# Experts ranked by token count on chip, their matrices fetched in rank order, and the extra items moved to places nine to eleven

## The chip, the core and the metric

The kernel runs on one NeuronCore of a Trainium2 chip. Its engines are TensorE (PE, with its weight loads PEld), VectorE (DVE), ScalarE (ACT), GpSimd (POOL) and SyncE (SP); each takes its own instructions strictly in the order of the program and waits at semaphores. The metric is the device time of one execution in microseconds.

## What is computed

2048 rows of 512 numbers are normalised and go through one of four experts each; the expert follows from the row's token id. All three matrices of an expert are the same 512 x 512 context matrix. Behind that stands a second normalisation and a block with low-rank routed adapters, which the change leaves alone.

```python
def _L0_xattn_ref(hidden_states, token_ids, Wg, Wu, Wd):
    ...
    expert_ids = jnp.minimum(tid // tokens_per_expert, E - 1)
    out = jnp.zeros_like(hidden_states)
    for e in range(E):
        g = jax.nn.silu(jnp.einsum('bsd,fd->bsf', hidden_states, Wg[e]))
        u = jnp.einsum('bsd,fd->bsf', hidden_states, Wu[e])
        y = jnp.einsum('bsf,df->bsd', g * u, Wd[e])
        out = jnp.where((expert_ids == e)[..., None], y, out)
    return out
...
x = x + jnp.tanh(g_xattn[0]) * _L0_xattn_ref(_layernorm(x, axis=-1), itok_BxS_13_99985, ctx_2048, ctx_2048, ctx_2048)
x = x + jnp.tanh(g_ffn[0]) * _L0_ffn_ref(_layernorm(x, axis=-1), ...)
```

## The kernel before, in words

**Items.** The kernel sorts the rows by expert on chip (a counting sort on VectorE, with matrix products on TensorE for the sums over partitions and for the permutation) and gathers them as 16 tiles of 128 rows. A tile in which another expert begins needs a second pass with that expert's matrix; there are three such extra passes, so 19 items in all. The extra items stand at places 1 to 3 (`EXTRA_AT = 1`), so that items 0 to 3 have the fixed keys 0 to 3, one expert each.

**An item's path.** GpSimd gathers its rows (`gather`); VectorE takes their statistics (`first_rows`, later `item_stats` and `item_aggregate`); GpSimd makes root and centre of them (`item_root`); ScalarE normalises (`norm`). The row block h is split into a high and a low half of 16 bits and transposed: for items 0 to 4 by TensorE (`transpose_h` there, then `hT_hi` on ScalarE and `hT_lo` on VectorE), from item 5 on by a DMA of SyncE's queue (`h_hi`, `h_lo`, then `transpose_h` of SyncE). TensorE computes z = h * ct in twelve matmuls (hi by hi, lo by hi, hi by lo). ScalarE makes `silu_of` z, VectorE multiplies (`activate`), both split the result (`act_hi`, `act_lo`), SyncE's queue transposes it (`transpose_act`), and TensorE computes y = act * ct in twelve matmuls (`product_y`). VectorE adds y to the rows (`add_product`). Here z0 is the z product of item 0, y0 its y product. From item 6 on a loop runs z of item q and y of item q-2 in turn, and each engine does its part of the items around q in one round.

**The matrices.** Each of the four matrices (1 MB in f32) comes through `ct_stage` and is split in two halves of rows into 16-bit high and low parts (`ct_hi` on ScalarE, `ct_lo` on VectorE), after a scale that follows from the sum of its squares (`ct_scales` on VectorE). For the first matrix ScalarE squares and sums; for the others TensorE multiplies the matrix by itself (`gram`) and VectorE takes the trace (`trace`). A product with ones (`total`) sums over partitions.

**The order at the start.** SyncE loads ids, gates and three matrices at once, the fourth after the first four gathers were issued. VectorE makes the row index (`row_index`) and two short tables and then goes into a handwritten order of calls, from `ct_scales` of the first matrix to the loop; the gate mask (`gates_of_rows`) stands in the middle of it. GpSimd issues four gathers and then alternates roots and gathers; `scale_tables`, which makes the scales of all items from the four matrices' scales, stands once, behind root 6. The weights W of the second block are loaded in the ramp, squared in rounds 8 and 9, scaled (`w_exponent`, `w_scales`) in rounds 10 and 11 and split from round 12 on. An extra item's product is stored over its gathered rows and added to its tile in rounds 11 to 13 (`add_extra`), where VectorE reads the tile's number from a table into a register (`target_of`, a `value_load`).

TensorE's own order at the start, several calls to a line, where the prediction walks along:

```python
transpose_h(0); keep_warm(WARM_BETWEEN); z_hi_by_hi(0, 0); z_lo_by_hi(0, 0); z_hi_by_lo(0, 0)
transpose_h(1); gram(3); z_hi_by_hi(1, 1); z_lo_by_hi(1, 1); transpose_h(2); z_hi_by_lo(1, 1)
...
z_hi_by_hi(2, 2); transpose_h(3); z_lo_by_hi(2, 2); z_hi_by_lo(2, 2); product_y(0, 0); transpose_h(4); z_hi_by_hi(3, 3)
...
product_y(1, 1); product_z(5, keys[5]); product_y(2, 2); product_y(3, 3)
```

## Time and profile before

| what | value |
|---|---|
| median of 3 runs | 199.44 us (199.04 to 199.58) |
| the profiled execution, its own time | 198.81 us |
| its span, first to last instruction | 197.1 us |
| mean granted TensorE clock | 0.971 of full speed |
| TensorE busy | 185.5 us (94%) |
| VectorE busy | 142.5 us (72%) |
| ScalarE busy | 111.9 us (57%) |
| GpSimd busy | 116.2 us (59%) |
| chain that ended last | TensorE 81%, GpSimd 7%, VectorE 5%, issue 3% |

The chain of waits follows the work that ended last back to the start; "issue" is time in which an engine waited for nothing that the profile shows. Times of rows are from the span's start. The 1.7 us between the execution's time and its span lie around the instructions. An engine's idle time outside the chain costs nothing by itself, but sets when others can start.

### The profile page before, as it was taken

The numbers are of one execution on the slowest core, as the hardware profiler recorded it, in microseconds if no ns is written. First come the engines' busy times: TensorE is split into PE (matmuls) and PEld (weight loads), VectorE is DVE, ScalarE is ACT, GpSimd is POOL, SyncE is SP. The second block draws the span as 40 slices with busy tenths as digits, with TensorE's granted clock in tenths as the row PEclk, the third lists the DMA queues.
The fourth block names the chain that finished last, engine by engine and source line by source line (L and its number), as shares of the span: only waits on it lengthen the run. The fifth ranks groups of instructions, "written<-read, shape, count | busy, mean of one in ns | idle before, by whom it ended". The sixth has DMA issues, their size and how long they took to land.

```text
span 197.1 us, 3762 instructions
## 1 busy us (share of the span) xinstructions
PE 185.5 (94%) x1085; PEld 107.6 (55%) x1085; DVE 142.5 (72%) x409; ACT 111.9 (57%) x208; POOL 116.2 (59%) x190
## 2 busy tenths in 40 slices
PE   6699899899999999999999999999999999999970
PEld 2374435344444454444444446667778777787750
DVE  5959889968866666998888664676767777676370
ACT  4563769465357765267665456354756777567310
POOL 5578856882566662233377654376776767765441
PEclk9966999999999999999999999999999999999995
DMA  2988426889799998456569997565989989889951
GB/s 86 365 297 276 148 74 168 219 167 185 145 212 214 180 222 188 92 105 117 106 137 216 205 239 200 85 175 151 114 131 131 139 125 124 135 124 131 127 91 72
DMA packets 59827, 31.63 MB, mean 161 GB/s; under 512 B 53105, under 2 KB 53105, under 8 KB 59810
## 3 DMA queue, kind: packets, MB, share of 16 engines
q1 hardware_dynamic: 54994, 18.58, 46.5%
q0 software_dynamic: 4816, 12.85, 30.5%
q8 instruction: 8, 0.13, 0.3%
q14 instruction: 9, 0.07, 0.1%
HBM read 10.71 MB, written 7.86 MB: 94 GB/s over the span
## 4 chain that ended last, share of the span: by engine, by line
PE 81%; POOL 7%; DVE 5%; issue 3%; ACT 1%; POOLq 1%
PE actT_ps L783 8%; PE y_ps L783 8%; PE ffn_b L783 6%; PE z_ps L783 6%; PE ffn_b L765 6%; PE ffn_a L765 6%; POOL xg L431 4%; PE actT_ps L788 4%; PE y_ps L788 4%; PE z_ps L788 3%; PE ffn_b L788 3%; PE ffn_b L769 3%; PE z_ps L765 3%; PE ffn_a L769 3%; PE y_ps L765 3%
## 5 line engine op out<-in xcount | busy, mean ns | idle before, releaser
L502 POOL DMA_INDIRECT out<-scaled,row_index x14 | 22.4, 1603 | 10.5 <-ACT scaled L611 4.9
L431 POOL DMA_INDIRECT xg<-x_rows,row_index x19 | 21.8, 1149 | 5.5 <-issue 4.2
L394 POOL TENSOR_SCALAR var_eps<-item_stats_t 128x1 f32<-128x1 f32 x19 | 6.9, 366 | 30.3 <-DVE item_stats_t L1116 30.0
L566 ACT ACTIVATE act_split<-act 128x512 f16<-128x512 f32 x19 | 11.9, 628 | 15.8 <-DVE act L1141 15.7
L765 PE MATMUL ffn_a<-w_split,hT 128*128 128x316 f16 x88 | 18.8, 298 | 0.0
L765 PE MATMUL ffn_b<-w_split,hT 128*128 128x314 f16 x88 | 18.4, 296 | 0.0
L444 POOL DMA_INDIRECT out<-xg,row_index x14 | 14.7, 1053 | 5.3 <-issue 3.0
L574 ACT ACTIVATE h<-xg,item_centre,item_rstd 128x512 f32<-128x512 f32 x18 | 14.5, 803 | 5.2 <-POOL item_centre L404 5.1
L783 PE MATMUL actT_ps<-ct_split,actT 128*128 (+1 forms) x72 | 17.0, 379 | 0.0
L783 PE MATMUL y_ps<-ct_split,actT 128*128 (+1 forms) x72 | 17.0, 379 | 0.0
L596 ACT ACTIVATE expd<-logits,neg_max 128x6 f32<-128x6 f32 x16 | 4.8, 300 | 19.8 <-DVE neg_max L1287 19.8
L587 ACT ACTIVATE h<-xg,centre,rstd 128x512 f32<-128x512 f32 x16 | 12.8, 802 | 3.5 <-POOL centre L491 3.5
L1146 DVE TENSOR_TENSOR act_split<-act,act_split 128x512 f16<-128x512 f32 x19 | 13.0, 683 | 1.3 <-ACT act_split L566 1.3
L1112 DVE BATCH_NORM_STATS2 bn<-xg 128x6 f32<-128x512 f32 x19 | 13.0, 687 | 1.0 <-DMA xg<-x_rows,row_index 1.0
L484 POOL TENSOR_SCALAR var_eps<-stats 128x1 f32<-128x1 f32 x16 | 6.8, 423 | 11.7 <-DVE stats L1119 11.6
L783 PE MATMUL ffn_b<-ct_split,hT 128*128 x56 | 13.2, 379 | 0.0
L783 PE MATMUL z_ps<-ct_split,hT 128*128 x56 | 13.2, 379 | 0.0
L397 POOL TENSOR_TENSOR item_rstd<-var_eps,minus_half 128x1 f32<-128x1 f32 x19 | 11.5, 603 | 1.6
L769 PE MATMUL ffn_b<-w_split,hT 128*128 128x314 f16 x44 | 11.8, 296 | 0.0
L769 PE MATMUL ffn_a<-w_split,hT 128*128 128x316 f16 x44 | 11.7, 296 | 0.0
L559 ACT ACTIVATE silu<-ffn_b,z_scale 128x512 f32<-128x512 f32 x9 | 6.1, 682 | 9.8 <-PE ffn_b L788 6.6
L783 PEld LDWEIGHTS y_ps<-ct_split,actT 128*128 128x128 f16 x72 | 7.0, 98 | 8.5
(227 smaller groups left out, 474.2 us busy)
## 6 DMA issues: line engine op xcount, KB each, us to landing
ct_stage<-ct SPq DMA_DIRECT2D x4, 1024.0 KB, 7.7
w_stage<-w_ffn SPq DMA_DIRECT2D x4, 315.0 KB, 3.7
hT<-h_split SPq DMA_TRANSPOSE x30, 3.7
xg<-x_rows,row_index POOLq DMA_INDIRECT x19, 3.9
actT<-act_split SPq DMA_TRANSPOSE x19, 3.8
out<-xg,row_index POOLq DMA_INDIRECT x16, 2.7
up_stage<-w_up SPq DMA_DIRECT2D x1, 224.0 KB
out<-scaled,row_index POOLq DMA_INDIRECT x14
```

The source lines that it names most:

```text
L431: nc.gpsimd.indirect_dma_start(cols(xg, q), None, x, bass.IndirectOffsetOnAxis(row_index[:, q:q + 1], 0)).then_inc(x_landed[q], 16)
L444: nc.gpsimd.indirect_dma_start(out, bass.IndirectOffsetOnAxis(row_index[:, q:q + 1], 0), cols(xg, q), None).then_inc(x2_stored, 16)
L502: nc.gpsimd.indirect_dma_start(out, bass.IndirectOffsetOnAxis(row_index[:, q:q + 1], 0), scaled[t % 3][:], None, compute_op=ALU.add).then_ ...
L566: nc.scalar.activation(act_split[q % 2][:, 0:D], act[:], ACT.Copy).then_inc(act_hi_ready, 1)
L574: nc.scalar.activation(h[:], cols(xg, q), ACT.Identity, bias=column(item_centre, q), scale=column(item_rstd, q)).then_inc(h_ready, 1)
L587: nc.scalar.activation(h2[:], cols(xg, tile_position(l)), ACT.Identity, bias=centre[:], scale=rstd[:]).then_inc(h2_ready, 1)
L765: nc.tensor.matmul(ps, h2T[turn][:, k], rhs(part), start=(k == 0 and part == 0), stop=False)
L769: return nc.tensor.matmul(ps, h2T[turn][:, KC + k], rhs(0), start=False, stop=(k == KC - 1))
L783: nc.tensor.matmul(ps[:], lhs[:, k], expert_weights(key, k, part), start=(k == 0 and part == 0), stop=False)
L788: last = nc.tensor.matmul(ps[:], lhs[:, KC + k], expert_weights(key, k, 0), start=False, stop=(k == KC - 1))
L1112: nc.vector.bn_stats(bn[:], cols(xg, q)).then_inc(bn_ready, 1)
L1146: tt(act_split[q % 2][:, D:], act[:], act_split[q % 2][:, 0:D], ALU.subtract).then_inc(act_lo_ready, 1)
```

## The change

The kernel ranks the four experts by their number of rows and sorts the rows in that order, so that items 0 to 3 all belong to the largest expert and items 4 to 7 to the two largest (`ITEM_GROUPS`). Only the first matrix is needed before item 4, the second before item 8, the third and the fourth from items 9 and 10 on. SyncE loads W first, waits for the order, reads the experts' numbers into registers and loads the matrices in rank order, in halves and spread over the ramp. All squares are ScalarE's; `gram` and `trace` are gone. The extra items stand at places 8 to 10, and their products are added straight onto their tiles, whose numbers VectorE loads into three registers ahead of its first row. W's squares, exponent and scales move to the start, the gate mask too. `scale_tables` runs three times, once for each group of items, each time as soon as its matrices have scales. GpSimd's order of gathers and roots changes. Stores of finished tiles begin some rounds earlier. `ct_total(s)` waits for both squares of matrix s and sums them on TensorE.

The core of the diff:

```diff
-WARM_UP = (2, 1, 2, 5)
-WARM_BETWEEN = 3
-EXTRA_AT = 1
-EXTRA_ADD_AT = 11
+WARM_UP = (8, 8)
+WARM_BETWEEN = 1
+EXTRA_AT = 8
...
+        ITEM_GROUPS = ((0, 4, (0,)), (4, EXTRA_AT, (0, 1)), (EXTRA_AT, ITEMS, (0, 1, 2, 3)))
...
+        def ranks_split_by(q):
+            if q < 4:
+                return 1
+            return min(S, max(2, q - EXTRA_AT + 2))
...
@@ SyncE @@
+            for k in range(KC):
+                load_w(k)
+            sp.wait_ge(order_ready, 1)
+            expert_of_rank = [order_of(0)]
+            load_ct(0, 0)
+            load_ct(0, 1)
+            expert_of_rank += [order_of(s) for s in range(1, S)]
...
+            sp.wait_ge(first_gathered, 1)
+            load_ct(1, 0)
+            load_ct(1, 1)
...
             transpose_act(0)
-            load_w(0)
-            load_w(1)
+            load_ct(2, 0)
             transpose_act(1)
-            load_w(2)
+            load_ct(2, 1)
             transpose_h(5)
             transpose_act(2)
             transpose_act(3)
...
@@ GpSimd, in scale_tables(group), and its main order @@
+                pool.wait_ge(z_scale_ready, len(ranks))
                 pool.wait_ge(tables_ready, 1)
...
             gather(0)
             gather(1)
-            gather(2)
-            gather(3)
             nc.gpsimd.memset(gathered_mark[:], 0.0).then_inc(first_gathered, 1)
             item_root(0)
+            gather(2)
+            item_root(1)
+            gather(3)
+            scale_tables(0)
+            item_root(2)
             gather(4)
-            item_root(1)
+            item_root(3)
             gather(5)
+            scale_tables(1)
+            item_root(4)
             gather(6)
...
@@ ScalarE @@
+            w_square(0)
+            w_square(1)
+            ct_square(0, 0)
+            ct_square(0, 1)
             ct_hi(0, 0)
             ct_hi(0, 1)
             hT_hi(0)
...
+            act_hi(1)
             hT_hi(3)
+            ct_square(1, 1)
             norm(4)
             silu_of(2)
+            act_hi(2)
             hT_hi(4)
+            ct_hi(1, 0)
             norm(5)
             h_hi(5)
+            ct_hi(1, 1)
             silu_of(3)
...
+                if q == 6:
+                    ct_hi(2, 0)
+                    ct_square(3, 1)
...
@@ TensorE @@
+            z_hi_by_hi(2, 0)
             transpose_h(3)
+            z_lo_by_hi(2, 0)
+            z_hi_by_lo(2, 0)
+            ct_total(1)
             product_y(0, 0)
+            z_hi_by_hi(3, 0)
             transpose_h(4)
+            z_lo_by_hi(3, 0)
+            z_hi_by_lo(3, 0)
+            product_y(1, 0)
             pe.wait_ge(tables_ready, 1)
             keys = {q: key_of(q) for q in (4, 5)}
...
                 product_z(q, key)
+                if q == 7:
+                    ct_total(3)
...
@@ VectorE @@
+            dve.wait_ge(tables_ready, 1)
+            targets = [dve.value_load(target_table[0:1, bass.ds(q, 1)], min_val=0, max_val=ITEMS - 1)
+                       for q in range(EXTRA_AT, EXTRA_AT + EXTRAS)]
...
+            w_exponent()
+            w_scales()
+            first_rows(0)
+            ct_scales(0)
+            first_rows(1)
+            first_norm()
             ct_lo(0, 0)
+            hT_lo(0)
             ct_lo(0, 1)
...
+                if q == 9:
+                    ct_lo(3, 0)
+                    ct_lo(3, 1)
```

## Rows read from the trace of the kernel before

**Rows 1.** Windows: start and end, length, busy time by engine, PEclk, DMA share, GB/s.

```profile
19.67:40.98 21.31, 19.34 (x106) 9.44 (x106) 19.16 (x41) 14.57 (x21) 15.58 (x25) 1.00 0.56 154
40.98:190.00 149.02, 148.89 (x881) 88.76 (x880) 107.99 (x302) 87.35 (x176) 84.89 (x131) 1.00 0.83 152
11.90:18.60 6.70, 6.49 (x31) 3.93 (x31) 5.24 (x13) 3.32 (x4) 5.61 (x7) 0.50 0.78 234
```

**Rows 2.** The chain of waits in order of time: start, length, what.

```profile
35.89 0.98 issue
...
51.72 1.73 PE z_ps L783 x8
...
72.78 1.75 PE z_ps L783 x8
```

**Rows 3.** Timeline: the Gram product between the first z products, on TensorE.

```profile
23.18 1.08 PE L735 MATMUL ffn_b<-ct_stage 128*128 128x128 bf16 x16
```

**Rows 4.** Timeline: from the counting matmuls to the first z product.

```profile
4.39 0.21 DVE L1066 TENSOR_TENSOR begun<-ffn_a,tile_starts 128x45 f32<-128x45 f32 x1 [0.41 <-PE ffn_a L706]
...
7.00 2.13 DVE L1086 TENSOR_SCALAR lo_onehot<-iota_row,slot_lo 128x128 f16<-128x128 f16 x12
...
9.52 0.18 DVE L1089 CAST row_index<-ffn_a 128x19 int32<-128x19 f32 x1 [0.38 <-PE ffn_a L715]
...
10.01 0.18 DVE L1096 CAST key_table<-item_key 128x19 int32<-128x19 f32 x1
...
14.54 0.69 DVE L1112 BATCH_NORM_STATS2 bn<-xg 128x6 f32<-128x512 f32 x1 [0.97 <-DMA xg<-x_rows,row_index]
...
19.67 2.76 PE L794 MATMUL z_ps<-ct_split,hT 128*128 128x512 f16 x12
```

**Rows 5.** Timeline of VectorE: the gate mask, first and last; the weight steps likewise.

```profile
38.68 0.21 DVE L1042 SCALAR_TENSOR_TENSOR reached<-ffn_a,row_slot 128x57 f32<-128x57 f32 x1
...
39.58 0.23 DVE L1104 TENSOR_SCALAR gate_mask<-gate_mask,gates_t 128x19 f32<-128x19 f32 x1
...
75.03 0.13 DVE L1177 COPY w_total<-ffn_a 128x1 f32<-128x1 f32 x1
...
82.31 0.15 DVE L1193 COPY hw<-w_scale 128x1 f32<-128x1 f32 x1
```

**Rows 6.** By line: register loads, VectorE's and TensorE's queue; ns min/median/max.

```profile
L1161 DVEq TENSOR_LOAD <-target_table x3: 450/741/778, 77.0 to 86.5; - x3
L1161 DVEq FUSED_REGOPS  x3: 190/190/216, 77.8 to 87.3; - x3
...
L799 PEldq TENSOR_LOAD <-key_table x30: 296/310/1046, 34.7 to 118.4; - x30
```

**Rows 7.** GpSimd: gathers by line and landing; centres (timeline); scale table (groups).

```profile
L431 POOL DMA_INDIRECT xg<-x_rows,row_index x13: 942/1159/1872, 10.0 to 57.5; - x13
...
DMA to landing us min/median/max: 3.4/4.4/5.9
...
20.66 1.11 POOL L404 TENSOR_SCALAR item_centre<-item_stats_t,item_rstd 128x1 f32<-128x1 f32 x1
...
25.50 0.26 POOL L404 TENSOR_SCALAR item_centre<-item_stats_t,item_rstd 128x1 f32<-128x1 f32 x1
...
L412 POOL TENSOR_SCALAR z_scale_of<-item_key,z_scale 128x15 f32<-128x15 f32 x4 | 1.4, 362 | 0.0
```

**Rows 8.** Groups, 19 to 52 us: count, busy us, mean ns, idle before.

```profile
L1008 DVE SCALAR_TENSOR_TENSOR ct_split<-ct_stage,ct_scale,ct_split 128x1024 f16<-128x1024 f32 x6 | 7.6, 1267 | 0.0
L574 ACT ACTIVATE h<-xg,item_centre,item_rstd 128x512 f32<-128x512 f32 x7 | 5.6, 806 | 2.3 <-POOL item_centre L404 2.2
L540 ACT ACTIVATE ct_split<-ct_stage,ct_scale 128x1024 f16<-128x1024 f32 x4 | 4.6, 1139 | 0.3 <-DVE ct_scale L1023 0.3
L566 ACT ACTIVATE act_split<-act 128x512 f16<-128x512 f32 x6 | 3.7, 625 | 3.1 <-DVE act L1141 3.0
L548 ACT ACTIVATE hT<-hT_ps 128x512 f16<-128x512 f32 x5 | 3.0, 590 | 4.0 <-PE hT_ps L774 4.0
L1141 DVE SCALAR_TENSOR_TENSOR act<-ffn_b,act_scale,silu 128x512 f32<-128x512 f32 x3 | 2.2, 750 | 1.4 <-ACT silu L559 1.4
```

**Rows 9.** By line: SyncE's transposes of act, ns of issue; landing in us.

```profile
L310 SPq DMA_TRANSPOSE actT<-act_split x19: 1231/1233/2109, 27.9 to 121.0; - x19
...
DMA to landing us min/median/max: 3.2/3.8/5.3
```

More of the change, by code:

```diff
@@ L266, in build_block, with group_of, fixed_key @@
         Z_TOP = 18
-        W_SPLIT_AT = W_SCALE_AT + 2
+        W_SPLIT_AT = 10
         W_TOP = 14
+        ITEM_GROUPS = ((0, 4, (0,)), (4, EXTRA_AT, (0, 1)), (EXTRA_AT, ITEMS, (0, 1, 2, 3)))
+        def group_of(q):
+            return len([first for first, last, ranks in ITEM_GROUPS if first <= q]) - 1
+        def fixed_key(q):
+            if q < 4:
+                return 0
+            return q - EXTRA_AT + 1 if EXTRA_AT <= q < EXTRA_AT + EXTRAS else None
+        def ranks_split_by(q):
+            if q < 4:
+                return 1
+            return min(S, max(2, q - EXTRA_AT + 2))
         S_TOTAL, S_INVERSE, S_W = 0, 1, 2
@@ L554, in silu_of @@
                     act_e.wait_ge(act_ready, q)
-                if q < S:
-                    act_e.wait_ge(z_scale_ready, q + 1)
-                elif q == S:
-                    act_e.wait_ge(z_table_ready, 1)
-                nc.scalar.activation(silu[:], z_banks[q % 2][:], ACT.Silu, scale=column(z_scale, q)
-                                     ).then_inc(silu_ready, 1)
+                key = fixed_key(q)
+                if key is None:
+                    act_e.wait_ge(z_table_ready, group_of(q) + 1)
+                    scale = column(z_scale, q)
+                else:
+                    act_e.wait_ge(z_scale_ready, key + 1)
+                    scale = column(rank_z_scale, key)
+                nc.scalar.activation(silu[:], z_banks[q % 2][:], ACT.Silu, scale=scale).then_inc(silu_ready, 1)
             def act_hi(q):
@@ L743, in total, with ct_total @@
                 last.then_inc(ct_totalled, 1)
-            def total_of(first, count):
-                return squares_ps[:, TOTALS_AT + first:TOTALS_AT + first + count]
-            pe.wait_ge(ct_squared, 2)
-            total(first_total_ps[:, 0:1], ct_squares[:, 0:1], ct_squares[:, S:S + 1])
-            gram(1)
+            def ct_total(s):
+                pe.wait_ge(ct_squared, 2 * s + 2)
+                total(squares_ps[:, TOTALS_AT + s:TOTALS_AT + s + 1], ct_squares[:, 2 * s:2 * s + 1],
+                      ct_squares[:, 2 * s + 1:2 * s + 2])
+            pe.wait_ge(rows_ready, 1)
+            pe.wait_ge(w_squared, 2)
+            for part in (0, 1):
+                last = nc.tensor.matmul(w_total_ps[:, 0:1], ones_f32[:],
+                                        column(w_squares, part), start=(part == 0), stop=(part == 1))
+            last.then_inc(w_totalled, 1)
             keep_warm(WARM_UP[0])
-            pe.wait_ge(rows_ready, 1)
-            pe.wait_ge(traced, 1)
-            total(total_of(1, 1), ct_squares[:, 1:2])
+            ct_total(0)
             keep_warm(WARM_UP[1])
-            gram(2)
-            keep_warm(WARM_UP[2])
-            pe.wait_ge(traced, 2)
-            total(total_of(2, 1), ct_squares[:, 2:3])
-            keep_warm(WARM_UP[3])
             def ffn_hi_passes(ps, turn, rhs, k):
@@ L1046, in count_reached, with step, need @@
             def count_reached(keys):
                 return nc.vector.tensor_reduce(keys[:], reached[:], axis=AX.X, op=ALU.add)
+            def step(ins):
+                steps[0] += 1
+                ins.then_inc(dve_step, 1)
+                return steps[0]
+            def need(done):
+                dve.wait_ge(dve_step, done)
             dve.wait_ge(ids_loaded, 16)
@@ L1076, in _ @@
[L1076 to L1080 removed]
+            copied = step(cp(size_copies[:].rearrange("p a s -> p (a s)"), sort_ps[:, S:3 * S]))
+            sizes, size_keys = size_copies[:, 0], size_copies[:, 1]
@@ L1137, in activate @@
                 dve.wait_ge(silu_ready, q + 1)
-                dve.wait_ge(act_scale_ready, min(q, S) + 1)
+                key = fixed_key(q)
+                if key is None:
+                    dve.wait_ge(act_table_ready, group_of(q))
+                    scale = column(act_scale, q)
+                else:
+                    dve.wait_ge(act_scale_ready, key + 1)
+                    scale = column(rank_act_scale, key)
                 if q:
                     dve.wait_ge(act_lo_ready, q)
-                nc.vector.scalar_tensor_tensor(act[:], z_banks[q % 2][:], column(act_scale, q), silu[:], ALU.mult,
-                                               ALU.mult).then_inc(act_ready, 1)
+                nc.vector.scalar_tensor_tensor(act[:], z_banks[q % 2][:], scale, silu[:], ALU.mult, ALU.mult
+                                               ).then_inc(act_ready, 1)
             def act_lo(q):
@@ L1311, in _ @@
             for q in range(FIRST_STEADY, ITEMS):
[L1312 to L1318 removed]
+                if q == 6:
+                    ct_scales(2)
+                if q == 8:
+                    ct_scales(3)
+                adds_extra = EXTRA_AT <= q - LAG - 1 < EXTRA_AT + EXTRAS
+                if not adds_extra:
+                    add_product(q - LAG - 1)
+                act_lo(q - 1)
+                if adds_extra:
+                    h_lo(q + 2)
+                    if q - LAG - 1 == EXTRA_AT:
+                        for ahead in range(q, ITEMS):
+                            dve.wait_ge(x_landed[ahead], 16)
+                    add_product(q - LAG - 1)
                 if q + 3 < ITEMS:
```

492 lines of the change are left out of this document (236 added, 256 removed).

## The prediction, as it was put on record

> **What bounds the kernel now.** I read the windows first, then the chain of waits in order of time, then the timeline of the first 40 us. From 40.98 us, where the second y product starts, to 190 us TensorE is busy 148.89 of 149.02 us at full clock [rows 1], and the chain runs from product to product of 2.59 us (the sixth z at 51.72, the tenth at 72.78) [rows 2]. Nothing that only relieves VectorE, ScalarE or GpSimd after 41 us can shorten that. The other lead is the ramp: up to the first product at 19.67, and from there to 40.98, where five z products, one y product, four transposes and a Gram product stand in 21.3 us. So I follow the change as a shift of TensorE's products: where its first z starts, what work lies between that and its tenth z, and how long it stands still in between. Behind the tenth z both kernels do the same products.
>
> For the kernel before: eighteen products (z0 to z9, y0 to y7) at 2.59 make 46.6; four transposes of about 0.47, one Gram product of 1.08 [rows 3] and two totals of 0.35 bring it to 50.3. 19.67 + 50.3 = 70.0; the tenth z stands at 72.78 in the chain, 72.6 in the timeline: 2.6 us of stalls, 0.98 of them the one at 35.89, in which two keys are loaded into registers [rows 2].
>
> **The start, step by step.** The sort. Before, 2.61 us lie between the first step behind the counting matmuls (4.39) and the first one-hot (7.00) [rows 4]. The new chain on VectorE has twelve dependent small steps there (copy, compare, count, start, part, sum, round, and then the ranks' starts and the extra tiles) where there were seven; such steps lie 0.19 to 0.30 apart. I get 3.6 us, and the row index at 10.50 instead of 9.52: +0.98. SyncE's wait for the order is not on the path: the order is out at about 6.3, one register load of about 1.1 and two half loads later the 1 MB are under way by 8.6 and land by about 13, before anyone can use them.
>
> What stands on VectorE between the row index and the first row's statistics. Before: two short tables, done by 10.19; then it waits for the row, which lands at 14.54 [rows 4]. After: the tables with their ranks (1.5 us by the same steps); the gate mask, moved here from 38.68 (39.58 + 0.23 - 38.68 = 1.13) [rows 5]; three register loads, moved from 77 to 87; the weight exponent and the weight scales, moved from 75.03 and from ahead of 82.31 (four and seven small instructions, 0.13 to 0.21 each and mostly dependent: 0.7 and 0.9) [rows 5]. The trace never shows three loads running. A load takes 0.45 to 0.78 us on VectorE, with the operations on its register 0.7 to 1.1; on TensorE's queue the shortest take 0.30, with theirs 0.5 [rows 6]. Three lie between 1.5 and 3.4; I take 2.55, one of 1.1 and two between. Sum: 10.50 + 2.5 + 2.55 + 1.6 = 17.1 for the first statistics. The row itself, gathered at about 11, is there by 14.5 to 15.5 (3.4 to 5.9 us to landing) [rows 7], so what was cover has become the path.
>
> From the statistics the old path took 5.1 us to the first product (14.54 to 19.67) [rows 4]. The new one: statistics 0.9, scales of the first matrix, which now come behind them, then two hi splits of 1.14 [rows 8] in ScalarE's order ahead of the copy of the transposed row (18.3 to 20.5, copy to 21.05). First z at 21.1: **+1.4**.
>
> **The work between.** The Gram product goes (-1.08 [rows 3]), a third total comes (+0.35): **-0.7**. The total of W moves ahead of the first product and costs nothing there: TensorE waits for VectorE anyway; if that cover were gone, 0.35. Extra items written straight onto their tiles spare VectorE three additions at a place where TensorE is full: nothing. Their later place (ninth to eleventh) changes which key a product reads, not its length. The key loads now stand behind a y product of 2.59 us, which hides them: the 0.98 is among the old stalls that I strike.
>
> **Stalls.** GpSimd gets the rows one at a time: before, four gathers were issued before the first root; now the third gather waits for the first root, the fifth for the third. Root 1.2 us, gather 1.16 plus 0.3, 3.6 to landing when little else moves [rows 7]. In TensorE's order:
> - the transpose of item 1 waits for its centre: 0.6 (1.6 if that centre meets a lo split on VectorE, where it took 1.11) [rows 7];
> - transpose of item 2: GpSimd goes through root, gather, root, gather, the first scale table (five dependent operations, 1.5 with steps of 0.2 to 0.36, the slowest of them in [rows 7]) and a root, some 8.5 us from the first statistics; normalised rows at 27.05, while TensorE is through its work at 25.1: 2.0;
> - the total of the second matrix stands ahead of the first y. It waits for ScalarE's second square, and that for the fifth row's gather (issued at about 26.5, landed 30.1), its statistics 0.9, activation 0.75, act's hi split 0.63, a copy 0.6 [rows 8] and the square, priced like a hi split with a sum read behind it, 1.24: 34.0, where TensorE is through at 32.35: 1.65;
> - transpose of item 4: GpSimd's second scale table stands ahead of root 4 and waits for the second matrix's scales. Total 0.35, scales 0.5, table 2.2, root 1.2, normalisation 0.8 [rows 8] make 5.0; y0 and a third of z3 cover 3.45: 1.5;
> - z4 waits for the second matrix's hi halves: silu, activation, hi split, copy, half, normalisation, its hi split, half, 5.9 us after that transpose on ScalarE; TensorE has 4.8 us of work: 1.15;
> - y2: SyncE has the transpose of h5 ahead of that of act 2. It issues for 1.23 once h5's lo half is there, and act 2 lands 3.8 us after its own issue [rows 9]: 2.3;
> - from there ScalarE, VectorE and GpSimd run behind by a loop of their own, statistics 0.9, root 1.3, normalisation 0.8, hi split 0.6, silu 0.65, activation 0.75, hi 0.65, lo 0.65 (silu and lo like hi) [rows 8], 6.3 us an item against TensorE's 5.18. The fourth matrix's total (behind z7) waits for a square at the end of ScalarE's round: 2.2. z10 waits for the fourth matrix's two lo halves, 1.27 each, in one round of VectorE: 1.7. Two smaller ones: 0.25.
>
> Together 13.35, where 2.6 stood before: **+10.75**. Sum: 1.4 - 0.7 + 10.75 = **+11.4**. From z10 on all matrices are split and TensorE is full again. The last stretch is unchanged. The profiled execution is 198.81 us (span 197.1, 1.7 around it); 198.81 + 11.4 = 210.2. It lies 0.6 below the median of the runs, which the forecast is given for: 199.44 + 11.4 = **210.8**. The unknown costs move it: the loads by -1.2 or +0.9, landings of 3.4 or 5.9 us in two places by -0.4 or +4.6, of which TensorE's stalls elsewhere take half, the centre of item 1 by +1. With sums of waits by hand, an overlap that I miss takes off more than I can name: 207 to 214.
>
> **Rivals.** *The backlog is made up.* Stalls up to y2 as summed, but ScalarE and VectorE have slack in the rounds after it, since two halves of ct a round are all that is added and before, ScalarE was busy 87.35 of 149.02 us and VectorE 107.99 [rows 1]: the last 4.15 go, and if the scale tables run beside other waits, another 4 or so. 199.44 + 7.3 = 206.7 down to 201.5. For it: no wait in the steady rounds of before is on the chain. Against it: the 6.3 us loop.
>
> *The ramp becomes TensorE-bound* (the other side): only one matrix is split before the first product instead of three, and VectorE and ScalarE are freed of some six halves of 1.27 and 1.14 us [rows 8] before 37 us. It decides if the register loads take 0.5 each and the row lands last: first z at 20 to 20.5, Gram gone, stalls below 2.6. 199.44 + 0.6 - 0.7 - 2.6 = 196.7, 195.5 to 198.5. Against it: the order in which GpSimd gathers.
>
> [...]
> [...]
>
> *No difference*: the start's +1.4 is paid by the Gram product and the key loads and the waits fall beside each other: 199.1 to 200.0.
>
> **How the numbers follow.** Forecast (207 to 214) 0.60; backlog made up (201.5 to 206.9) 0.20; clock beyond it 0.06; TensorE-bound ramp 0.11; within 0.3% 0.03. Slower by over 0.3%: 0.60 + 0.20 + 0.06 = 0.86; within 0.3% (0.6 us, about what a measurement of this kernel can tell from no change): 0.03; faster: 0.11. The range 201.5 to 216 holds the first two and most of the third, 0.84.
>
> **What would show it.** Right: first statistics near 17 with VectorE waiting for nothing but register loads ahead of it; first z near 21; TensorE idle ahead of the transposes of items 2 and 4, of the totals and of y2; GpSimd waiting for the second matrix's scales; z10 near 84; from there full TensorE to the end. Wrong: first statistics at the row's landing, or TensorE without stalls over 1 us from 25 us on (then the faster rival); stalls up to y2 but none at the last total and at z10 (backlog made up); granted clock below 1.00 after 21 us (the clock).

## The result and the profile after

The changed kernel takes 213.66 us (213.14 to 213.83, 4 runs), the kernel before, on the same chip, 199.24 us (198.77 to 199.58): a ratio of 1.072, 95% interval 1.069 to 1.0751. It is slower by 14.4 us; 11.4 were forecast. The profiled execution took 213.69 us, its span is 211.9 us, 14.8 us more than the 197.1 of before (the profiled run of before lay 0.4 us below the median of this comparison). Some runs of e2, e10 and e11 lie over 1.5% above the fastest run of the same kernel, and the times given for these three are medians of their other runs.

The windows of the kernel after (start and end, length, busy time by engine with counts, PEclk, DMA share, GB/s), cut at z0, at z10 (the forecast's "tenth z": items count from zero) and at 119.61 us behind that:

```profile
0.00:21.66 21.66, 15.04 (x69) 7.22 (x69) 15.46 (x81) 10.44 (x14) 10.04 (x35) 0.84 0.59 192
...
21.66:84.54 62.88, 51.60 (x244) 23.61 (x245) 42.98 (x80) 38.75 (x59) 34.94 (x67) 1.00 0.68 156
84.54:204.15 119.61, 117.07 (x726) 73.73 (x727) 83.40 (x249) 68.37 (x146) 70.92 (x102) 1.00 0.81 142
```

The windows of the kernel before between the same products:

```profile
19.67:72.78 53.11, 51.13 (x255) 24.18 (x256) 41.52 (x81) 34.20 (x52) 33.82 (x61) 1.00 0.79 177
```

Read by the three stretches of the forecast: the first z starts at 21.66 and not at 19.67, +1.99. From it to z10 lie 62.88 us and not 53.11, +9.77, although TensorE is busy for about as long in both (51.60 and 51.13, some records of either may be missing): the difference is idle time. From z10 to the end of the span lie 211.9 - 84.54 = 127.36 us, where 197.1 - 72.78 = 124.32 lay before, +3.04. The sum is 14.80. (72.78 is the place of z10 in the chain of waits of before; its timeline has 72.64, which makes the last two +9.91 and +2.90.) TensorE's clock is 1.00 in both long stretches.

Where TensorE stands still is in its timeline of the kernel after (start, length, what; in brackets the idle time ahead of it and what ended it), from the first z on:

```profile
21.66 1.90 PE L848 MATMUL z_ps<-ct_split,hT 128*128 128x512 f16 x8 [0.47 <-ACT hT L609]
24.47 0.66 PE L828 MATMUL hT_ps<-ident,h 128*128 128x128 f32 x4 [0.91 <-ACT h L637]
28.49 0.66 PE L828 MATMUL hT_ps<-ident,h 128*128 128x128 f32 x4 [1.63 <-ACT h L637]
35.16 0.61 PE L798 MATMUL ffn_a<-ct_squares,ones_f 128*128 128x1 f32 x4 [1.26 <-ACT ct_split L588]
40.46 0.66 PE L828 MATMUL hT_ps<-ident,h 128*128 128x128 f32 x4 [1.22 <-ACT h L637]
46.64 2.76 PE L848 MATMUL z_ps<-ct_split,hT 128*128 x12 [1.20 <-ACT ct_split L601]
50.82 1.89 PE L837 MATMUL y_ps<-ct_split,actT 128*128 128x512 f16 x8 [1.42 <-DMA actT<-act_split]
56.56 0.61 PE L798 MATMUL ffn_a<-ct_squares,ones_f 128*128 128x1 f32 x4 [0.41 <-ACT ct_split L588]
69.35 0.61 PE L798 MATMUL ffn_a<-ct_squares,ones_f 128*128 128x1 f32 x4 [1.69 <-ACT ct_split L588]
84.54 1.90 PE L837 MATMUL z_ps<-ct_split,hT 128*128 x8 [1.54 <-DVE ct_split L1055]
92.73 1.90 PE L837 MATMUL actT_ps<-ct_split,actT 128*128 x8 [0.24 <-DMA actT<-act_split]
104.72 1.90 PE L837 MATMUL actT_ps<-ct_split,actT 128*128 x8 [1.22 <-DMA actT<-act_split]
107.70 1.90 PE L837 MATMUL z_ps<-ct_split,hT 128*128 x8 [0.22 <-issue]
129.29 1.90 PE L837 MATMUL z_ps<-ct_split,hT 128*128 x8 [0.69 <-issue]
```

Behind the first line, nine waits up to z10 come to 11.28 us. Six of the nine have ScalarE's normalised rows or squares at the other end, two a half of a matrix (z4 and z10), and one, y2, waits for a transpose. Four small ones stand behind z10. Of all these the kernel before shows only its 0.98 ahead of the fifth z [rows 2] and some shorter ones.

What came late ahead of the first product is in VectorE's timeline of the kernel after:

```profile
10.88 0.18 DVE L1155 CAST row_index<-ffn_a 128x19 int32<-128x19 f32 x1 [0.38 <-PE ffn_a L783]
...
13.92 0.23 DVE L1173 TENSOR_SCALAR gate_mask<-gate_mask,gates_t 128x19 f32<-128x19 f32 x1 [0.34 <-DVE gate_mask L1171]
16.11 0.16 DVE L1246 COPY w_total<-ffn_a 128x1 f32<-128x1 f32 x1 [1.96 <-issue]
...
17.70 0.14 DVE L1262 COPY hw<-w_scale 128x1 f32<-128x1 f32 x1
17.76 0.68 DVE L1179 BATCH_NORM_STATS2 bn<-xg 128x6 f32<-128x512 f32 x1
```

The row index is at 10.88 (9.52 before, [rows 4]); tables and gate mask end at 14.15; then VectorE stands for 1.96 us in which nothing is waited for but its own queue, the three register loads; the steps of w's scale follow to 17.84, and the first statistics come directly behind them, with no bracket: the row is there and waits.

### The profile page after: what moved, and what is told of

It reads as the page before. It is cut to its first block, busy times and chain, and to the rows that moved or that the text cites. A ratio compares the mean times of both kernels' runs of the same rounds, so it can differ in the third digit from the quotient of the medians.

```text
span 211.9 us, 3745 instructions
## 1 busy us (share of the span) xinstructions
PE 185.3 (87%) x1048; PEld 105.8 (50%) x1048; DVE 143.6 (68%) x412; ACT 117.8 (56%) x220; POOL 117.9 (56%) x204
## 4 chain that ended last, share of the span: by engine, by line
PE 48%; DVE 14%; POOL 11%; issue 10%; ACT 8%; DMA 4%; DVEq 1%; POOLq 1%; ACTq 0%
PE ffn_b L819 6%; PE ffn_a L819 5%; PE actT_ps L837 3%; DVE act L1214 3%; PE ffn_b L823 3%; PE z_ps L837 3%; PE z_ps L819 3%; ACT h L637 3%; PE ffn_a L823 3%; PE y_ps L819 3%; PE y_ps L837 2%; DMA actT<-act_split 2%; DVE bn L1179 2%; POOL item_rstd L434 2%; POOL xg L484 2%
## 5 line engine op out<-in xcount | busy, mean ns | idle before, releaser
L431 POOL TENSOR_SCALAR var_eps<-item_stats_t 128x1 f32<-128x1 f32 x19 | 8.0, 419 | 31.7 <-DVE item_stats_t L1183 31.0
L484 POOL DMA_INDIRECT xg<-x_rows,row_index x19 | 20.4, 1072 | 6.3 <-issue 3.5
L1201 DVE TENSOR_TENSOR h_split<-h,h_split 128x512 f16<-128x512 f32 x14 | 9.7, 690 | 13.8 <-ACT h_split L644 13.6
L819 PE MATMUL ffn_a<-w_split,hT 128*128 128x316 f16 x88 | 18.8, 298 | 0.0
L496 POOL DMA_INDIRECT out<-xg,row_index x14 | 14.8, 1059 | 5.4 <-issue 2.2
L601 ACT ACTIVATE ct_split<-ct_stage,ct_scale 128x1024 f16<-128x1024 f32 x8 | 9.0, 1135 | 5.6 <-DVE ct_scale L1065 5.6
L837 PEld LDWEIGHTS actT_ps<-ct_split,actT 128*128 128x128 f16 x72 | 7.0, 100 | 9.7 <-issue 3.1
```

Source lines behind the costliest of these rows:

```text
L484: nc.gpsimd.indirect_dma_start(cols(xg, q), None, x, bass.IndirectOffsetOnAxis(row_index[:, q:q + 1], 0)).then_inc(x_landed[q], 16)
L496: nc.gpsimd.indirect_dma_start(out, bass.IndirectOffsetOnAxis(row_index[:, q:q + 1], 0), cols(xg, q), None).then_inc(x2_stored, 16)
L819: nc.tensor.matmul(ps, h2T[turn][:, k], rhs(part), start=(k == 0 and part == 0), stop=False)
L837: nc.tensor.matmul(ps[:], lhs[:, k], expert_weights(key, k, part), start=(k == 0 and part == 0), stop=False)
L1201: tt(h_split[q % 3][:, D:], h[:], h_split[q % 3][:, 0:D], ALU.subtract).then_inc(h_lo_ready, 1)
```

## The experiments

Each kernel below is the changed kernel with the edit shown, and each was timed beside the kernel before. The first four undo one suspected cost apiece.

**Register loads and w's scales later on VectorE** (e1):

```
-            targets = [dve.value_load(...) for q in range(EXTRA_AT, EXTRA_AT + EXTRAS)]   # ahead of the first statistics
+                if adds_extra: load_target(q - LAG - 1 - EXTRA_AT)                        # in its own round
...
-            w_exponent(); w_scales()        # ahead of first_rows(0)
+            w_exponent(); w_scales()        # ahead of activate(2)
```

> VectorE's three register loads are put off to the rounds that use them, and the weight exponent and scales to its wait ahead of item 2's activation; all else is as in the changed kernel. Theory (what stands on VectorE ahead of the first row's statistics is the path): the first statistics begin at the row's landing, 15 to 15.8 us instead of 17.76, the first z near 19.5 to 20 instead of 21.66, and since GpSimd's roots and gathers follow from the first statistics, the end moves by as much: -1.6 to -2.3 us, 211.4 to 212.1. Rival (the ramp is set by later waits, the gathers and the matrices' arrival, so that the start has cover): the first z moves, the tenth z does not, 213.2 to 213.8.

Measured: 212.12 us (211.31 to 213.24), -1.5. The first z is 1.8 us earlier. TensorE's timeline of this kernel:

```profile
19.87 1.90 PE L848 MATMUL z_ps<-ct_split,hT 128*128 128x512 f16 x8 [0.47 <-ACT hT L609]
26.36 0.66 PE L828 MATMUL hT_ps<-ident,h 128*128 128x128 f32 x4 [2.42 <-ACT h L637]
```

The wait ahead of item 1's transpose is gone and that ahead of item 2's has grown from 1.63 to 2.42, for GpSimd's gathers set its time; z10 starts at 82.19, 2.35 us earlier. That trace is of the fastest of four runs, which lie 1.9 us apart, so the gain is known only roughly. The start's cost is of the kind that the forecast said: work ahead of the first statistics in VectorE's order.

**Gathers of items 2 and 3 ahead of the first root** (e2):

```
             gather(0); gather(1)
+            gather(2); gather(3)
             item_root(0)
-            gather(2)
             item_root(1)
-            gather(3)
```

> GpSimd issues the gathers of items 2 and 3 before the first root, as in the kernel before; nothing else moves. Theory (the rows arrive too late because a gather waits behind roots): the transpose of item 1 stands some 1 us earlier and that of item 2 some 1.5 to 2 us, the fifth gather goes out 1 us earlier, the total of the second matrix comes 1 us earlier and so does all behind it: -0.8 to -1.5 us, 212.1 to 212.9. Rival (the early stalls are covered by what ScalarE does for the second matrix): no change, 213.4 to 213.9.

Measured: 210.9 us (two runs, 210.43 and 211.4), -2.7, more than expected. In its trace the wait ahead of item 1's transpose is gone, item 2's shrinks to 0.88, and z10 starts at 82.62, 1.9 us earlier. Behind z10 the trace is 1.3 us shorter as well (126.1 us to its end instead of 127.4), which the theory did not have; the wait ahead of y11 is 0.47 there instead of 1.22. With two runs the size of the gain is uncertain.

**The second scale table behind the fifth item's root** (e3):

```
-            scale_tables(1)
             item_root(4)
+            scale_tables(1)
```

> GpSimd's second scale table stands behind root 4 instead of ahead of it. Theory (root 4 waits through the table for the second matrix's scales, and ScalarE, in order, waits with it): the transpose of item 4 comes at 39.1 instead of 40.46, ScalarE's copies and splits behind it 2 us earlier, the second matrix's hi halves with them, y2 2 us earlier: -1.5 to -2.3 us, 211.3 to 212.1. Rival (a stall of TensorE that only moves to the next wait, the transposes in SyncE's queue): -0.0 to -0.5 us, 213.1 to 213.7.

Measured: 210.9 us (210.69 to 211.52), -2.8, rather more than expected. The 1.22 ahead of item 4's transpose goes, and so does the wait ahead of z4, which was caused by the same late rows: the hi halves of the second matrix stand behind them on ScalarE. Two lines of one engine's order, swapped, are worth a fifth of the whole loss.

**h_lo behind the statistics also in the extras' rounds** (e4):

```
                 if adds_extra:
-                    h_lo(q + 2)
...
-                elif not adds_extra:
+                else:
                     h_lo(q + 2)
```

> In the three rounds that add an extra product VectorE's lo half of h goes back behind the statistics. The trace of the changed kernel shows 2.4 us of stalls behind the tenth z (0.4, 0.2, 1.4, 0.4) that the prediction did not name, and a loop of 5.65 us an item there: statistics, root, normalisation, hi half, lo half, addition, statistics. Theory: with the statistics ahead of the lo half the loop is open and the stalls go, -1.8 to -2.6 us, 211.0 to 211.9. Rival (the stalls are a backlog that the rounds before hand on, or slow transposes in the DMA queues): -0.0 to -0.6 us, 213.0 to 213.7.

Measured: 212.46 us (212.39 to 213.62), -1.2, between the two. The small waits at 92.73 and 129.29 go, but the one of y11 stays (by the order of the products the wait at 104 us is y11's; the expectations call it y10's). From TensorE's timeline and VectorE's:

```profile
104.47 1.90 PE L837 MATMUL actT_ps<-ct_split,actT 128*128 x8 [1.34 <-DMA actT<-act_split]
```

```profile
94.32 0.75 DVE L1226 SCALAR_TENSOR_TENSOR xg<-y_ps,y_scale,xg 128x512 f32 x1 [0.58 <-DMA xg<-x_rows,row_index]
```

The second line names what the first does not: the first extra addition, whose target is known only from a register, waits until every gathered row has landed.

**The stores of the first tiles later** (e8, on top of e4):

```
-                    if t < 4 and n >= 13 or n >= EXTRA_AT + EXTRAS + 6 and tile_position(t) + 1 <= n - 4:
+                    if n >= EXTRA_AT + EXTRAS + 6 and tile_position(t) + 1 <= n - 4:
```

> As the run with h_lo behind the statistics in the extras' rounds (212.46 us), and the stores of the first four tiles' rows begin some rounds later, behind the last gathers, as the other tiles' do. Theory (the transposed activation that lands 5 us after its issue is slowed by these stores, whose packets share the DMA engines with it; y10 waits for it 1.4 us): that wait and those of the next rounds go, 210.8 to 211.4 us. Rival (gathers and the transposes themselves fill the engines, or the wait is VectorE's and ScalarE's): 212.1 to 212.8 us, the wait of 1.4 us ahead of y10 still there.

Measured: 213.02 us (211.88 to 213.46), no gain on 212.46. The wait ahead of y11 is gone, but one of 1.09 stands two y products sooner (ahead of y9, at 93.47). So holding the stores back moves the wait and wins no time.

**The gathers sooner** (e9, on top of e4): from the fifth root on two gathers to a root, so that none is left behind the third scale table.

```
             item_root(4)
-            gather(6)
-            item_root(5)
-            gather(7)
...
+            gather(6); gather(7)
+            item_root(5)
+            gather(8); gather(9)
...
+            item_root(8)
+            gather(14); gather(15)
```

> As the run with h_lo behind the statistics in the extras' rounds (212.46 us), and GpSimd gathers the rows of items 7 to 18 two to a root from the fifth root on, so that the last four are no longer queued behind the third group's scale tables. Theory (these tables occupy GpSimd for 6.2 us, the last four gathers and the next root come out behind them, share the DMA engines with the transposes at 85 to 95 us, and the first added extra waits for the last row; that is what keeps the transposed activation of item 10 for 5 us): the wait of 1.4 us ahead of y10 and VectorE's wait for the landed rows go, 210.6 to 211.4 us. Rival (the transposes are slow there by themselves, or the gathers only meet other transposes sooner): 212.0 to 213.0 us with a wait of over 1 us ahead of a y between y8 and y11.

Measured: 210.36 us (210.22 to 210.38), -2.1 on e4 and -3.3 on the changed kernel. TensorE has no wait over 0.2 us between z10 (84.40) and the end of the routed products, and from z10 to the end of its span (208.5) lie 124.1 us, as before the change (124.32). This is the chain of waits of the *changed* kernel in order of time, in the place concerned (start, length, what):

```profile
82.06 1.13 POOL z_square L476
83.19 1.20 POOL gated_power L478
84.84 1.13 POOL xg L484
...
88.25 0.27 POOL item_centre L441
88.55 0.82 ACT h L637
...
99.42 5.04 DMA actT<-act_split
104.72 1.90 PE actT_ps L837 x8
```

GpSimd works at the third scale table from 78.45 to 84.67, 6.2 us. Two of its multiplications (`z_square`, `gated_power`) take 1.13 and 1.23 us, and each ends about when one of VectorE's two lo halves of the fourth matrix does; the next one, of the same size and behind these halves, takes 0.21. From the timelines of VectorE and GpSimd:

```profile
81.87 2.45 DVE L1055 SCALAR_TENSOR_TENSOR ct_split<-ct_stage,ct_scale,ct_split 128x1024 f16<-128x1024 f32 x2
...
84.46 0.21 POOL L480 TENSOR_TENSOR y_scale<-z_square,gated_power 128x11 f32<-128x11 f32 x1
```

The last four gathers and the next root stand behind the table; the rows come late, normalisation and rounding follow late, and y11 waits for a transpose that lands 5.04 us after its issue. Sooner gathers with h_lo put back remove all of it, although the table still takes 6.2 us there (78.30 to 84.52). Which share is the late root's and which the transfers' own is not told apart.

**SyncE without the order** (e5): the matrices are fetched by a fixed index.

```
-            sp.wait_ge(order_ready, 1)
...
-                return sp.value_load(order_table[0:1, bass.ds(s, 1)], ...)
+                return s
```

> SyncE neither waits for the order of the experts nor loads it into registers: the matrices are fetched by a fixed index as early as SyncE reaches them, so that the products use matrices which don't follow the rank order (the chip-made order, and only that, is left out of the fetch; the sort still runs). Theory (the first product waits for VectorE's queue and the first item's rows, not for the first matrix): within 0.7 us of the changed kernel's 213.7 us. Rival (the order is on the path to the first matrix's total or scale): 211.5 to 212.7 us, the first product 1 to 2 us earlier.

Measured: 213.86 us (213.62 to 214.28): no change. The first z is at 21.64. Waiting for the order costs nothing at the start, as forecast. TensorE's timeline of this run shows one thing more:

```profile
21.64 3.58 PE L847 MATMUL z_ps<-ct_split,hT 128*128 128x512 f16 x8 [0.47 <-ACT hT L608]
```

The same eight matmuls take 1.90 us in the changed kernel. TensorE had waited 3.09 us ahead of item 0's transpose here (1.48 in the changed kernel), and its granted clock is 0.57 from 21.64 to 25.64. The next waits take this up: the one ahead of item 1's transpose is gone, and item 2's transpose is at 28.46 as against 28.49.

**The four edits together** (e6 = e1 to e4):

> All four edits of the runs before at once: register loads and w's scales later on VectorE, the gathers of items 2 and 3 ahead of the first root, the second group's scale tables behind the fifth item's root, h_lo behind the statistics in the extras' rounds. Theory (each removes a wait of its own, in series on TensorE): the gains of the single runs add up, 1.5 + 1.0 + 2.8 + 1.2 = 6.5 us less than the changed kernel, 207.2 us, 206.2 to 208.2. Rival (they shorten the same stretch ahead of the same later wait, so that the wait behind it grows by what was won): no better than the best of them and a little, 209.0 to 210.5 us, with longer idle stretches ahead of the fourth matrix's total and of z10.

Measured: 207.05 us (206.42 to 207.37), -6.6, inside the range; the rival is out. The sum of 6.5 took 1.0 for e2, though. With its 2.7 the single gains come to 8.2, so they add up only in part. The traces say the same: z10 is 2.35, 1.92, 2.83 and 0 us earlier in the four single runs, 7.1 together, and 5.80 earlier here. The wait of 0.91 ahead of item 1's transpose, for one, goes in e1 and in e2 alike and can be won only once. That the forecast of 207.2 was met so closely is partly luck.

**Three further waits of TensorE** (e7, on top of e6): the fourth matrix's total behind y5, z8 to z10 with the pass that needs the matrix's lo half last, and act 2's transpose ahead of h5's.

```
-                if q == 7: ct_total(3)
                 product_y(q - LAG, y_key)
+                if q == 7: ct_total(3)
...
+                if 8 <= q <= 10:
+                    ...product_of_parts(hi, hi); product_of_parts(lo, hi); z_hi_by_lo(q, key)
...
+            transpose_act(2)
             transpose_h(5)
-            transpose_act(2)
```

> The four edits together, and three more for the waits left on the matrices and on the transposes: the fourth matrix's total behind y5 in place of ahead of it, the products z8 to z10 begun with the two passes that need no rounding rest of the matrix (the pass with the rest last), and SyncE's transpose of item 2's activation ahead of item 5's rows. Theory (TensorE waits there for work that is merely queued in that order): 1.85 us ahead of the total, 1.7 ahead of z10 and 1.5 ahead of y2 go for the most part, 3.5 to 5 us less than the four edits alone, about 202.2 to 203.7 if those give 207.2. Rival (the loop from statistics to the transposed activation has a round longer than TensorE's 5.2 us there, so what is won in front is waited out behind): at most 2 us less than the four edits alone.

Measured: 206.24 us (205.88 to 206.5), -0.8, the rival. All three waits are gone or nearly so, and others have taken their place. TensorE's timeline of this kernel:

```profile
50.12 0.61 PE L798 MATMUL ffn_a<-ct_squares,ones_f 128*128 128x1 f32 x4 [1.98 <-ACT ct_split L588]
...
86.07 1.90 PE L837 MATMUL actT_ps<-ct_split,actT 128*128 x8 [1.53 <-DMA actT<-act_split]
97.84 1.90 PE L837 MATMUL actT_ps<-ct_split,actT 128*128 x8 [1.24 <-DMA actT<-act_split]
```

What y2 no longer waits, the third matrix's total waits (0.41 in the changed kernel, 1.98 here), and what z10 no longer waits y9 and y11 behind it do.

**The queues reordered** (e10, on top of e7): no work added or taken away. The main lines:

```
 DVE: first_rows(2) ahead of ct_lo(0, 0); first_rows(6) ahead of add_product(0); first_rows(7), w_exponent(), w_scales() behind add_product(1)
 ACT: norm(2) ahead of ct_square(1, 0); ct_square(1, 1) behind silu_of(1); ct_square(2, 1) ahead of silu_of(4)
 POOL: scale_tables(0) behind item_root(2); gathers two to a root from item_root(4) on
 SP: load_ct(3, 0) ahead of transpose_h(6), load_ct(3, 1) behind it
```

> On top of the run with the matrix waits moved (206.24 us): statistics of items 2, 6, 7 and 8 earlier in VectorE's order, w's scales later still, the squares of the second halves of matrices 2 and 3 placed into ScalarE's idle stretches, the fourth matrix fetched a transpose sooner, GpSimd's gathers two to a root from the fifth root on and its first table behind the third root. No work is added or taken away. Theory (TensorE's 12.3 us of idle stretches there come from the order of the queues alone, ScalarE and VectorE being busy for 65 and 76 of 100): about 1 us ahead of the third transpose, 1.2 and 2 us ahead of the totals and half of the 4.7 us ahead of the products y and z10 go, 198.5 to 201.5 us, as fast as the kernel before or nearly. Rival (a round of transposed activations takes longer than TensorE's 5.2 us whatever the order, so what is won in front is waited out behind): 203.5 to 206 us.

Measured: 206.23 us (four runs, 205.26 to 207.17), no better than e7; just above even the rival's range. The waits for ScalarE's squares are gone. The chain of waits shows what replaced them:

```profile
29.61 9.24 DMA xg<-x_rows,row_index
...
51.56 9.00 DMA actT<-act_split
60.82 3.58 PE y_ps L842 x8
```

A gather and a transposed activation take 9 us to land, where the medians are 3.9 and 3.8 in the changed kernel; the DMA engines' mean share is 1.27 from 32 to 36 us and 1.29 from 52 to 56. TensorE waits 2.47 us ahead of z6 and 2.50 ahead of y4, and y4's first eight matmuls then take 3.58 us instead of 1.90. The window says why:

```profile
60.00:64.00 4.00, 3.18 (x8) 1.27 (x9) 0.00 (x0) 3.35 (x5) 1.38 (x2) 0.61 1.16 277
64.00:68.00 4.00, 4.00 (x19) 1.78 (x18) 2.70 (x6) 1.84 (x4) 0.00 (x0) 0.97 0.39 116
```

The granted clock is 0.61 in the first 4 us, 0.50 from 61.00 to 64.00, and 0.97 in the next 4. Its waits of 2.47 and 2.50 us end 5.3 us apart.

**The transfers spread** (e11, on top of e10): gathers 7 to 10 between item_root(5) and item_root(6), none in the next two rounds, the fourth matrix fetched as in the changed kernel, item 6's statistics back behind act_lo(3), silu_of(0) and act_hi(0) earlier.

```
 POOL: item_root(5), gather(7), gather(8), gather(9), gather(10), item_root(6), item_root(7), item_root(8), gather(11), gather(12)
```

> As the run with the queues reordered (206.72 us), but with the transfers kept apart: the gathers of items 7 to 10 in the stretch from 37 to 44 us, in which the DMA engines were 0.4 to 0.8 busy, none in the next two rounds, the fourth matrix fetched as late as in the changed kernel, item 6's statistics back behind act_lo(3), and ScalarE's silu and rounding of item 0 ahead of the square and the transposed row beside them. Theory (that run lost its gain to DMA engines that the first matrices, the gathers and the transposes fill from 28 to 64 us: a gather took 9.2 us and a transposed activation 9.0 us there, and TensorE waited twice 2.5 us): 201.5 to 204.0 us, no transfer in that stretch over 6 us, no idle stretch over 2 us. Rival (each transfer moved meets another one, the engines being full over the whole ramp): 205.0 to 207.5 us.

Measured: 208.36 us (three runs, 208.3 to 209.32), 2.1 more than e10, and a miss of both. One transfer met others after all, as the rival had it. From the chain of waits, and the windows from 60 us on:

```profile
56.13 9.42 DMA actT<-act_split
65.81 3.56 PE actT_ps L839 x8
```

```profile
60.00:64.00 4.00, 2.66 (x12) 1.07 (x11) 1.44 (x4) 3.62 (x6) 2.49 (x2) 1.00 1.24 182
64.00:68.00 4.00, 2.19 (x6) 0.92 (x7) 2.50 (x4) 2.90 (x5) 2.89 (x4) 0.73 1.18 209
```

TensorE waits 3.15 us ahead of y5 here, and the clock falls again behind that wait.

**All matrices early, by a fixed index** (e12, on top of e11): as in e5 the order is left out, and the 4 MB are under way by 19 us.

```
-            load_ct(2, 0) ... load_ct(3, 1)       # between the transposes
+            for s in (2, 3): load_ct(s, 0); load_ct(s, 1)      # behind the first gathers
```

> As the run with the transfers spread (208.84 us), but all four matrices are fetched by a fixed index, without waiting for the chip-made order, so that the products use matrices which don't follow the rank order: the first two at once behind w, the other two as soon as the first gathers are out (about 16.6 us), so that none of their 4 MB is left for the stretch from 28 to 64 us. Theory (in that stretch the DMA engines are the limit, because the rank order puts the matrices' transfers there beside gathers and transposes; the waits of 2.3, 1.7, 0.7 and 3.3 us, and TensorE's lower clock behind the longest, go with them): 199.0 to 203.0 us. Rival (the loop of statistics, rounding and transposes is too long there by itself): 205.5 to 209.0 us, waits of 2 us and more ahead of y products still there.

Measured: 205.05 us (204.79 to 207.21), -3.3 on e11, outside both ranges. With the matrices' transfers out of the stretch from 28 to 64 us the wait ahead of z6 goes, but y5's stays: TensorE's timeline, the window behind that wait, and the queues' shares of the DMA engines from 56 to 64 us (packets, MB, share):

```profile
64.33 1.90 PE L837 MATMUL actT_ps<-ct_split,actT 128*128 x8 [3.38 <-DMA actT<-act_split]
```

```profile
64.00:68.00 4.00, 3.67 (x20) 2.14 (x21) 1.92 (x7) 2.50 (x5) 3.33 (x5) 1.00 1.06 285
```

```profile
q1 hardware_dynamic: 1969, 0.49, 69.0%
q0 software_dynamic: 160, 0.52, 43.7%
```

Here SyncE's queue carries only transposes, and 0.49 MB of them with 0.52 MB of gathered rows fill the engines. So the matrices' place is worth some 3.3 us of e11's time. That transposes beside gathers hold the rest fits this stretch, but no run shows it for the whole. In e7's order no wait from 52 to 64 us exceeds 0.35 us, at a DMA share of 0.92 to 1.15. An order that keeps all three kinds apart was not found. None of these kernels reaches the 199 us of the kernel before; e7 and e10, at 206.2, are the fastest of those that follow the rank order.

## Why the prediction was right, and where it was not

*The start.* Forecast +1.4, measured +1.99. The sort was taken 0.38 too short (row index at 10.88, forecast 10.50), and the tables with the gate mask 0.77 too short (3.27 us from there to 14.15, forecast 2.5, where the two parts named come to 2.63). The register loads, for which no row stood, took 1.96 of the 1.5 to 3.4 in the bounds (2.55 taken). The first statistics are at 17.76 instead of 17.1, and the path behind them was sized right: 3.90 us to the first z, 4.0 forecast. e1 shows the mechanism: without these steps the first statistics wait for the row again, at 15.05, and z0 is at 19.87.

*Work and stalls from z0 to z10.* Forecast +10.05 (10.75 of stalls less 0.7 of work), measured +9.77. Term by term (idle time before the instruction, forecast in brackets): transpose of item 1 0.91 (0.6), of item 2 1.63 (2.0), second total 1.26 (1.65), transpose of item 4 1.22 (1.5), z4 1.20 (1.15), y2 1.42 (2.3), fourth total 1.69 (2.2), z10 1.54 (1.7), the smaller ones 0.41 (0.25). Every wait is there with the releaser that was named, and z10 starts at 84.54 (84.0). The mechanism was right, but the closeness of the total is partly luck: the waits come to 11.28 instead of 13.35, and those of before to 1.98 instead of 2.6, so they grew by 9.30 and not by 10.75; TensorE's busy time rose by 0.47 instead of falling by 0.7. The two errors nearly cancel. The terms given for the second matrix's square add up to 34.2 and not to 34.0, which would have made that wait 1.85; it was 1.26. The largest error of size is y2: act 2's transpose was issued behind h5's, as forecast, but it landed 3.2 us after its issue (47.52 to about 50.7), not the 3.8 of the median [rows 9]. e3 shows that transpose 4 and z4 are one cause, not two; the forecast had priced them apart.

*Behind z10: the step that failed.* "From z10 on all matrices are split and TensorE is full again" is wrong by 3.04 us. That sentence counted only the matrices. Two moves of the change lay in the same rounds and were costed at nothing: GpSimd's third scale table, now 6.2 us right ahead of the last four gathers, and h_lo put ahead of the statistics in the three extras' rounds. The runs show both: h_lo back gives 1.2 us (e4), the gathers out from behind the table 2.1 more (e9), and then the stretch is as long as before the change. The cover that the prediction took for granted, "at a place where TensorE is full", was gone, because the loop that the prediction had put down for the rounds ahead went on here. VectorE's rounding of the activation comes every 5.65 us in the extras' rounds of the kernel after, where TensorE needs 5.18 for an item:

```profile
93.05 0.69 DVE L1219 TENSOR_TENSOR act_split<-act,act_split 128x512 f16<-128x512 f32 x1 [0.70 <-ACT act_split L629]
...
98.70 0.69 DVE L1219 TENSOR_TENSOR act_split<-act,act_split 128x512 f16<-128x512 f32 x1 [0.70 <-issue]
...
104.35 0.69 DVE L1219 TENSOR_TENSOR act_split<-act,act_split 128x512 f16<-128x512 f32 x1 [0.70 <-ACT act_split L629]
```

In e4 the round from 98.47 to 103.22 takes 4.75 us, below TensorE's.

*The sum.* 1.99 + 9.77 + 3.04 = 14.8 where 1.4 + 10.05 + 0 = 11.4 were forecast. Nine tenths of the miss are the stretch behind z10; the errors up to z10 nearly cancel. Of the 14.4 us the four edits give back 6.6 (e6), and e9's gathers gave back 2.1 on top of e4; both together were not run. What is left, 5 to 6 us, is seen as waits of TensorE on halves, squares and transposes. Taking three of these away (e7) won only 0.8, for others took their place, so the account of this part rests on the timeline and not on a run that gets it back.

*The rivals.* The backlog made up: not so, the last total and z10 still wait, 1.69 and 1.54 us. The TensorE-bound ramp: not so, TensorE is busy 51.60 of 62.88 us. No difference: no. The clock: the 0.06 of the chances and the upper end of the range to 216 rest on an estimate of the author's, 212 to 217 us, worked out from the 6.70 us at a granted clock of 0.50 in the kernel before [rows 1] (3.35 us a time, less what the stalls absorb). The changed kernel's trace shows no such cost: the clock stays at 1.00 from 21.66 to 204.15 through waits of up to 1.69 us, so it has no part in the result. Between z0 and 190 us it did fall in three other traces: in e5 (0.57 over 4 us behind a wait of 3.09, taken up by the next waits; and 0.69 from 68 to 72 us behind one of 1.76, where z10's wait is 0.63 instead of 1.54 and z10 starts at 85.00 instead of 84.54), in e10 (0.61 in one window of 4 us, behind two waits of 2.5) and in e11 (0.73 from 64 to 68 us, behind one of 3.15). e12's wait of 3.38 us and e1's of 2.42 left it at 1.00. What parts these cases the runs do not show.

## What to carry to other kernels

A change that makes one order known late (here the experts' ranks) moves work in many queues. Here waiting for that order cost nothing at the start (e5); what cost were steps moved in front of others in the order of VectorE (e1, 1.5 us) and of GpSimd (e2 and e3, 2.7 and 2.8). So price the start, but also each engine's queue for the steps that now stand ahead of someone else's. Swapping two lines on GpSimd gave back 2.8 us, and the four small reorderings 6.6 of 14.4, with the same work. Where a stretch is said to be "full again", check first that the loop feeding it has slack there; and when waits on engines are cleared by moving transfers, look at the DMA engines' share in that stretch before: it was 0.91 and 1.23 during e10's waits of 2.47 and 2.50 us, and 1.29 during e11's of 3.15.

## What the runs showed of the hardware

Three register loads from a table on VectorE, in a row, took 1.96 us of its queue. Two of GpSimd's multiplications of 128x11 took 1.13 and 1.23 us beside VectorE's splits, and one behind them 0.21. A gather and a transpose in e10 and a transpose in e11, over whose time the DMA engines' mean share was 1.04, 1.13 and 1.09, took 9.24, 9.00 and 9.42 us to land, against medians of 3.9 for gathers and 3.8 for transposes of act in the changed kernel; in 8 us of e12, 0.49 MB of transposes took 69% of the engines' time and 0.52 MB of gathered rows 44%. TensorE's granted clock fell behind a wait of 3.09 us and behind one of 1.76 (e5, 0.57 and 0.69 over 4 us), behind two of 2.47 and 2.50 (e10, 0.61) and behind one of 3.15 (e11, 0.73), but not behind one of 3.38 (e12) or one of 2.42 (e1), nor behind the waits of up to 1.69 in the changed kernel; eight matmuls took 3.46 to 3.58 us instead of 1.90 where it had fallen.
